# Cross-attention on one core: the tail products of up to three neighbouring PV steps issued ahead of their small products

## The reference

```python
q = _split_heads(hidden_states @ w_q, HEADS)
k = _split_heads(text @ w_k, HEADS)
v = _split_heads(text @ w_v, HEADS)
out_text = _merge_heads(_sdpa(q, k, v))
k_ip = _split_heads(ip_h @ w_k_ip, HEADS)
v_ip = _split_heads(ip_h @ w_v_ip, HEADS)
out_ip = _merge_heads(_sdpa(q, k_ip, v_ip, mask=mask_ip))
out = out_text + IP_SCALE * out_ip
out = out @ w_out + b_out
out = out + residual
```

## Time and profile before

| | |
|---|---|
| median of 3 runs | 709.34 us (707.8 to 711.19) |
| profiled execution | 710.03 us, of which the span of the trace 708.0 |
| TensorE busy | 685.1 us, 97% |
| TensorE weight loads | 633.3 us, 89% (beside the matmuls) |
| VectorE busy | 534.3 us, 75% |
| ScalarE, GpSimd busy | 291.0 us, 215.0 us |
| granted TensorE clock | 0.988 of full speed over the span |

### The profile page before, as it was taken

The page is one execution under the profiler, slowest core; times in us unless marked ns, Lnnn a source line. Parts: engine busy times, 40 slices in busy tenths (PEclk is TensorE's granted clock), DMA queues, the critical chain, the costliest instruction groups (busy, mean ns, idle before and its releaser), DMA issues.

```text
span 708.0 us, 19244 instructions
## 1 busy us (share of the span) xinstructions
PE 685.1 (97%) x6570; PEld 633.3 (89%) x6570; DVE 534.3 (75%) x1689; ACT 291.0 (41%) x636; POOL 215.0 (30%) x371
## 2 busy tenths in 40 slices
PE   6998999999999999999999999999999999999987
PEld 4787678989899999999998999999999999899876
DVE  3344468797879788887978787878888797978773
ACT  1132353351617262534435161726353442516160
POOL 5312006042423324150504242332415050424233
PEclk9999999999999999999999999999999999999989
DMA  9979616444436262534444353626353444434320
GB/s 297 379 212 213 152 37 142 130 105 111 123 83 163 67 173 77 147 84 140 100 133 103 105 130 77 171 67 168 82 142 90 134 101 121 112 82 118 80 64 37
DMA packets 52512, 89.40 MB, mean 126 GB/s; under 512 B 9440, under 2 KB 23520, under 8 KB 52460
## 3 DMA queue, kind: packets, MB, share of 16 engines
q1 hardware_dynamic: 51024, 86.09, 45.3%
q10 hardware_dynamic: 1068, 1.66, 0.9%
q0 software_dynamic: 384, 1.18, 0.8%
HBM read 39.21 MB, written 10.62 MB: 70 GB/s over the span
## 4 chain that ended last, share of the span: by engine, by line
PE 84%; SPq 5%; DMA 4%; DVE 3%; issue 1%; ACTq 1%; ACT 1%; POOL 0%; DVEq 0%
PE psum L1086 38%; PE psum L1147 9%; PE psum L1193 9%; PE psum L1172 5%; PE psum L1177 5%; SPq L414 4%; PE psum L1016 3%; PE psum L1201 3%; PE psum L1202 2%; PE psum L1216 2%; PE psum L954 2%; PE psum L1046 1%; PE psum L1199 1%; DMA q_stack<-mask_scratch 1%; DMA k_stack<-k_lo 1%
## 5 line engine op out<-in xcount | busy, mean ns | idle before, releaser
L570 POOL TENSOR_TENSOR attn<-o_parts 128x128 f32<-128x128 f32 x160 | 73.0, 457 | 418.3 <-DVE o_parts L901 388.0
L860 DVE TENSOR_REDUCE neg_max<-psum 128x2 f32<-128x292 f32 x320 | 144.6, 452 | 48.8 <-PE psum L1147 48.5
L1086 PE MATMUL psum<-wo_both,at_hi 128*128 128x320 f32 x640 | 153.6, 314 | 0.0
L1147 PE MATMUL psum<-k_stack,q_stack 104*128 104x154 f32 x640 | 113.6, 288 | 5.5 <-DMA q_stack<-mask_scratch 3.5
L1086 PE MATMUL psum<-xt_hi,wq_hi 128*128 128x256 f32 x400 | 114.6, 287 | 1.1 <-DVE q_lo L852 1.1
L1086 PE MATMUL psum<-xt_lo,wq_hi 128*128 128x256 f32 x400 | 111.7, 279 | 0.0
L1086 PE MATMUL psum<-xt_hi,wq_lo 128*128 128x256 f32 x400 | 111.5, 279 | 0.0
L1086 PEld LDWEIGHTS psum<-wo_both,at_hi 128*128 128x128 f32 x640 | 110.1, 189 | 0.0
L888 DVE TENSOR_TENSOR p_lo<-psum,p_hi 128x512 f16<-128x512 f32 x160 | 107.8, 682 | 2.8 <-ACT psum L714 2.7
L712 ACT ACTIVATE p_hi<-psum 128x512 f16<-128x512 f32 x160 | 95.2, 595 | 29.7 <-PE psum L1172 29.5
L1193 PE MATMUL psum<-v_tail,p_tail 128*128 128x264 f32 x320 | 102.4, 401 | 1.8 <-ACT p_tail L716 0.9
(11 more groups left out here) (96 smaller groups left out, 1268.3 us busy)
## 6 DMA issues: line engine op xcount, KB each, us to landing
q_stack<-q_hi SPq DMA_DIRECT2D x128, 96.0 KB
x_in<-in_x SPq DMA_DIRECT2D x16, 640.0 KB, 5.3
x_res<-in_x SPq DMA_DIRECT2D x16, 640.0 KB, 5.5
out<-out_sb SPq DMA_DIRECT2D x32, 320.0 KB
q_stack<-q_hi SPq DMA_DIRECT2D x128, 64.0 KB
q_stack<-q_lo SPq DMA_DIRECT2D x60, 96.0 KB
q_stack<-q_lo SPq DMA_DIRECT2D x60, 64.0 KB
q_stack<-aux_a SPq DMA_DIRECT2D x48, 64.0 KB, 2.4
```

The source lines that it names most:

```text
L570: nc.gpsimd.tensor_tensor(cols, o_parts[:, qt, 0:4, :], o_parts[:, qt, 4:8, :], ALU.add).then_inc(att_half, 1)
L860: nc.vector.tensor_reduce(dst[:, :, 0], src[:, :, 0:TEXT], AX_X, ALU.max, negate=True)
L1086: last = nc.tensor.matmul(ps, l(c), r(c), start=(i == 0), stop=(i == len(terms) - 1))
L1147: last = nc.tensor.matmul(scores[sc % 2][:, i * CTX:(i + 1) * CTX], q_stack[0:ROW_MAX, query_slot(h), P * qt:P * (qt + 1)], k_stack[batch] ...
```

## The change

On TensorE alone, PV steps that follow one another in the list without another step between are taken as a run of up to three. At the first step of the run the tail products of all its steps are issued, each into its own general bank behind its own waits, and then the small products of the first, the second and the third. With this list there is one run of three in a block, PV(1,1), PV(2,0), PV(2,1), and one of two, PV(3,0), PV(3,1). The other five PV steps stand alone. The lists of all engines, and the semaphores and their counts, are as before.

```diff
+TAILS_AHEAD = 3
+            def neighbours(order, at):
+                run = []
+                while len(run) < TAILS_AHEAD and at < len(order) and order[at][1] == "PV":
+                    run.append(tuple(order[at][2]))
+                    at += 1
+                return run
...
-                for stage, kind, args, gen, sc in it.steps():
+                order, tails = it.steps(), []
+                for at, (stage, kind, args, gen, sc) in enumerate(order):
...
                     if kind == "PV":
+                        run = neighbours(order, at)
+                        for g, qt in run if at not in tails else ():
+                            if isinstance(t, int) and t == 1 and (g, qt) == (0, 0):
+                                pe.wait_ge(s_vc, 5)
+                                pe.wait_ge(s_vsplit, 3 * V_PARTS)
+                            if qt == 0:
+                                pe.wait_ge(exp_done, t * ST_ALL - ST_ALL + 1 + max(ST_TURN[(g, u)] for u in range(3)))
+                                pe.wait_ge(p_split, t * 10 - 10 + 2 * g + 2)
+                            ahead = run.index((g, qt))
+                            free_general(it, gen + ahead)
+                            nc.tensor.matmul(product_1[it.general_bank(gen + ahead)][:, 0:8, :],
+                                             p_tail[:, -g % P_SLOTS, P * qt:P * (qt + 1)],
+                                             v_tail[batch][:, g, :].rearrange("p (e d) -> p e d", d=VW), start=True, stop=False)
+                            tails.append(at + ahead)
                         g, qt = args
-                        if isinstance(t, int) and t == 1 and (g, qt) == (0, 0):
-                            pe.wait_ge(s_vc, 5)
-                            pe.wait_ge(s_vsplit, 3 * V_PARTS)
-                        if qt == 0:
-                            pe.wait_ge(exp_done, t * ST_ALL - ST_ALL + 1 + max(ST_TURN[(g, u)] for u in range(3)))
-                            pe.wait_ge(p_split, t * 10 - 10 + 2 * g + 2)
-                        free_general(it, gen)
                         queries = slice(P * qt, P * (qt + 1))
-                        nc.tensor.matmul(product_1[it.general_bank(gen)][:, 0:8, :], p_tail[:, -g % P_SLOTS, queries],
-                                         v_tail[batch][:, g, :].rearrange("p (e d) -> p e d", d=VW), start=True, stop=False)
                         for j in range(4):
```

## The result

The changed kernel took 720.85 us (median of 4 runs, 716.48 to 722.46), the kernel before 710.06 in the same count of runs (707.8 to 711.19): a ratio of 1.0167 on record, 95% interval 1.0133 to 1.02 (the two medians divided give 1.0152). It is slower by clearly more than the half per cent that a measurement tells from no change, and by the amount forecast (1.6%, 720.7 us). The profiled execution took 721.98 us with a span of 719.1, against 710.03 and 708.0. One execution of the kernel before, in a later series, took 824.15 us at a granted clock of 0.757 and stands in no comparison here.

What follows compares the result with a forecast made beforehand. TensorE was taken as the bound, busy 685.1 of 708.0 us. Losses of 14 x 0.70 + 0.88 + 0.64 = 11.3 us on the median of 709.34 gave 720.7 us, range 716.5 to 724.5.

Steps and rivals of the forecast that it cites:

- The gain: TensorE, three tails per block behind a tail: each 0.45 us in place of 0.52, saving 0.22 us per block.
- The bound of 0.52 (no gain): TensorE's runs: if a tail behind a tail costs 0.52 us, the loss is 0.84 per block, time 722.8.
- The delay of PV(1,1): First run: PV(1,1) complete 0.9 us later, so VectorE stands for a microsecond before its reciprocal, later work queued behind.
- The two waits: Second run: PV(3,0)'s tail waits for p_lo, PV(3,1)'s for PV(2,0)'s bank; about 0.9 us of waiting and restarts per block.
- No third wait: Behind the second run: PV(4,0)'s tail at 307.64 finds p_lo ready at 306.76; everything after just 0.70 us later.
- The rival by which moments of idleness between groups of matmuls make the clock swing: TensorE's gaps in each block drop its clock, costing 27 us, time 748; chance 0.04.
- 14 x 0.70 in the loop: The 14 ordinary blocks: each loses 0.70 us, 0.22 saved against about 0.9 of waiting and restarts.
- 0.88 in the first block: First block: small products stand behind PV(2,1)'s tail, which waits for PV(1,0)'s bank; a loss of 0.88 us.
- 0.64 in the last: Last block: PV(4,0)'s tail already waited for p_lo of ST(4,1), which moves by 0.64 us.

Runs made afterwards that it cites:

- experiment 1: Against the kernel before, only the run of three PV(1,1), (2,0), (2,1) has its tails ahead; 716.26 us, ratio 1.0116.
- experiment 2: Against the changed kernel, at most two tails ahead: PV(1,1) with (2,0), (2,1) alone, (3,0) with (3,1); 711.47 us, ratio 1.0042.
- experiment 3: The changed kernel with p_lo of ST(3,1) put ahead of PV(1,1)'s normalisation in VectorE's list; 712.14 us, ratio 1.0068.
- experiment 6: Against the kernel before, only the run of three, with p_lo of ST(3,1) ahead of PV(1,1)'s normalisation in VectorE's list; 707.66 us, ratio 0.9984.
- experiment 4: Against the kernel before, PV(1,1) alone, tails of (2,0) and (2,1) together, then (3,0) and (3,1) together; 705.87 us, ratio 0.9971.

## Why the prediction was right

**The gain.** Expected 0.45 for a tail behind a tail, measured 0.447 (1.34 for three). The bound of 0.52 (no gain) is out.

**The delay of PV(1,1).** The reciprocal was to come 1.89 after the first tail and VectorE to stand for a microsecond; it came at 1.88 (306.33 to 308.21), after 1.02 of idle time. Its wait in all grew from 7.8 to 22.4 us, as forecast (over 20).

**The two waits.** PV(3,0)'s tail expected 3.45 after the first, measured 3.48. First small product of the second run 4.74, measured 4.72. ST(4,2) 5.43, measured 5.41, against 4.73 in rows 3: a loss of 0.68 up to there, where 0.70 was forecast, and 0.66 over the whole period as a mean of 13. Experiments 1 to 3 show that these are the causes, and 3 and 6 that their seat is VectorE's order. PV(3,0)'s tail waits in 15 of the 16 blocks (0.37 to 0.40 us, 12 of them put down to p_lo and 3 without a name), not in the first; PV(3,1)'s loads wait in all 16.

**No third wait.** PV(4,0)'s tail came 7.71 after the first, before 7.03, a difference of 0.68: nothing new behind the second run.

**The clock.** It stayed at 1.00 in the loop, through four periods with two waits each. The rival by which moments of idleness between groups of matmuls make the clock swing is out there; the rule of the Trainium skill behind it (TensorE: Matmul & The Clock Gate, "A second HAM failure mode: psum-queue depth-cycling") is not borne out for gaps of some 0.4 us with dense work between them. In the first block it is another matter, and the forecast has no term for it. The first 8 us from PV(1,1)'s tail on, in the kernel before, in the changed one and in its second profile:

```profile
106.36:114.36 8.00, 7.11 (x92) 6.02 (x91) 6.20 (x20) 3.80 (x8) 6.25 (x14) 1.00 0.98 213
...
107.56:115.56 8.00, 5.47 (x51) 4.15 (x50) 3.73 (x12) 2.38 (x6) 4.00 (x9) 0.79 1.02 239
...
106.19:114.19 8.00, 6.17 (x72) 5.02 (x71) 4.73 (x15) 3.42 (x7) 5.30 (x12) 0.79 0.99 231
```

At 0.79 the clock was at 1.2 GHz for part of these 8 us, in both profiles of the change and in none of the other eight. TensorE had stood for 2.49 and 1.83 us before PV(2,1)'s tail. That the wait brought the clock down is not shown: in experiments 4 and 6 it stood for 1.81 and 1.95 us at the same place, and the clock stayed at 1.00.

**Where the sum was right by luck.** It was made of 14 x 0.70 in the loop, 0.88 in the first block and 0.64 in the last. The difference of the two spans, 11.1 us, is made otherwise:

| stretch | before | after | difference |
|---|---|---|---|
| start to PV(1,1) of the first block | 106.36 | 107.56 | +1.20 |
| to PV(1,1) of the second block | 39.95 | 42.55 | +2.60 |
| 13 periods | 499.83 | 508.46 | +8.63 |
| to PV(1,1) of the last block | 37.47 | 37.04 | -0.43 |
| to the end | 24.39 | 23.49 | -0.90 |

The loop's part was 5% too large (0.70 for 0.66 per block). The first row is the start, which moves by more than that between executions.

In the first block the tail of PV(2,1) waits for a bank whose release hangs on GpSimd: VectorE's product into o_parts waits there for GpSimd to have added the parts before it (2.01 us in the kernel before, 3.26 after), and GpSimd's first addition waits for the DMA of the bias. Before and after:

```profile
106.90 0.45 POOL L570 TENSOR_TENSOR attn<-o_parts 128x128 f32<-128x128 f32 x1 [30.25 <-DMA bias<-in_L_xattn_b_out]
...
109.35 0.45 POOL L571 TENSOR_TENSOR attn<-o_parts 128x128 f32<-128x128 f32 x1 [30.63 <-DMA bias<-in_L_xattn_b_out]
111.11 1.25 PE L1204 MATMUL psum<-v_tail,p_tail 128*128 128x264 f32 x2 [2.49 <-DVE o_parts L905]
```

That tail starts 2.30 us behind PV(1,1)'s in one profile of the kernel before (108.66 in rows 5) and 3.16 in the other, 3.55 and 2.89 in those of the changed one: this part is the execution and not the change. Counted from that tail to PV(1,1) of the second block, the executions agree: 37.65 and 37.51 before, 39.00 and 38.98 after. So the change costs 1.3 to 1.5 us there, and 0.88 was forecast. The missing 0.5 or so goes with the fallen clock: from PV(2,1)'s tail to PV(4,0)'s it takes 7.64 and 7.54 us in the first block and 6.81 in the loop, while in experiment 1, at a clock of 1.00, it takes 6.72 and 6.64. By these distances an estimate for the clock is some 0.7 us.

In the other direction the last two stretches gave something back. In the last block PV(4,0)'s tail was 6.95 behind PV(1,1)'s against 6.33 (683.61 to 689.94), so 0.62 late where 0.64 was forecast; but before, the clock had fallen behind it, and after it had not:

```profile
704.00:710.00 6.00, 4.56 (x42) 4.37 (x42) 3.27 (x9) 1.75 (x4) 3.56 (x6) 1.00 0.00 1
```

The window that answers to it is in rows 6, at 0.72, which the forecast took as it was. In the second profile of the kernel before the clock stayed at 1.00 there, and this stretch took 22.84 us. The second profile of the change has 23.48, which is the forecast 0.64 more. So the fall was worth 1.6 us (24.39 less 22.84) of one execution.

The period ahead of the last block is no measure of the change. TensorE stands there for a DMA, that of the transposed row maxima. In the kernel before, in the changed one and in experiment 3:

```profile
681.70 0.50 PE L1172 MATMUL psum<-q_stack,k_stack 120*128 120x256 f32 x2 [0.76 <-DMA q_stack<-aux_b]
...
693.68 0.50 PE L1182 MATMUL psum<-q_stack,k_stack 120*128 120x256 f32 x2 [0.69 <-DMA q_stack<-aux_b]
...
681.56 0.51 PE L1183 MATMUL psum<-q_stack,k_stack 120*128 120x256 f32 x2 [2.59 <-DMA q_stack<-aux_b]
```

The stretch took 37.47 and 38.62 us in the two profiles of the kernel before, 37.04 and 36.97 in those of the change. The clock does not order these lengths either: 37.61 at 1.00 in experiment 3, 37.20 at 0.91 in experiment 4. What sets this stretch stays open.

That these parts cancel within 0.3 us is luck, and so is the agreement of the medians to 0.2 us (720.85 for 720.7): the same kernel gave 718.48 in its second series. The loop alone gives 16 x 0.66 = 10.6 us, and that part was forecast by its mechanism.

## What to carry to other kernels

Grouping like products on the bounding engine saves the transitions between them, but it also moves the moment at which the first of the group is complete, and that delays whatever stands behind its consumer in an engine that works in order. Before grouping, look in the consumer's timeline for the first product that the consumer takes up well after it is complete, and begin the group there: the same grouping begun one step later, at such a product, gained 0.14 us per block where this one lost 0.66. And where a gain of 0.07 us hangs on a transition, the period of the loop in a trace shows it, while the times of whole executions need a dozen runs.

## What the runs showed of the hardware

A restart behind a wait costs more than the wait: a tail that a semaphore released took 0.54 or 0.55 us to the next product instead of 0.45 (310.50 to 311.05 in the changed kernel). The weight loads fit this: a tail's first float32 load (0.19 us long) began 0.12 us ahead of its matmul behind float32 work (299.79 for 299.91), 0.03 behind small products (300.67 for 300.70) and 0.01 behind a wait (309.80 for 309.81).

Executions of one kernel differ by 1% in parts that lie outside the loop (106.36 and 106.71 us to PV(1,1) of the first block in the kernel before, 24.39 and 22.84 from that of the last block to the end), while the period of the loop at one place repeats to 0.02 us. That is finer than the times, and made eight kernels comparable from one profile each.
